# The second cross-attention's preparation done inside the self-attention before it

## The reference

```python
x = x + _L0_attn_ref(_layernorm(x), ...)            # state space
x = x + _L0_xattn_ref(_layernorm(x), ctx_768, ...)  # cross-attention, 16 heads of 64
x = x + _L0_ffn_ref(_layernorm(x), ...)             # 8 experts
x = x + _L1_attn_ref(_layernorm(x), ...)            # self-attention, 16 heads of 8, distance bias
x = x + _L1_xattn_ref(_layernorm(x), ctx_768, ...)  # second cross-attention
x = x + _L1_ffn_ref(_layernorm(x), ...)             # 8 experts
```

```python
q = layernorm(x) @ Wq; k = ctx[:, :124] @ Wk; v = ctx[:, :124] @ Wv     # 16 heads of 64
ki = ctx[:, 124:] @ Wk_ipa; vi = ctx[:, 124:] @ Wv_ipa                  # 4 "image" tokens
out = softmax(q k^T / 8) v + softmax(q ki^T / 8) vi
x = x + out @ Wo + bo
```

## Time and profile before

| | |
|---|---|
| Median of 3 runs | 705.98 us |
| Lowest, highest | 703.78, 708.40 us |
| Profiled execution | 707.48 us, of which the span from the first to the last instruction is 705.7 us |
| Mean granted TensorE clock | 0.961 of full |
| Self-attention | 302.24 us to 406.16 us of the span |
| Opening of the second cross-attention | 407.51 us to 433.72 us of the span |

### The profile page before, as it was taken

The page is one execution under the profiler, slowest core; times in us unless marked ns, Lnnn a source line. Parts: engine busy times, 40 slices in busy tenths (PEclk is TensorE's granted clock), DMA queues, the critical chain, the costliest instruction groups (busy, mean ns, idle before and its releaser), DMA issues. The chain is left out here.

```text
span 705.7 us, 13252 instructions
## 1 busy us (share of the span) xinstructions
PE 639.6 (91%) x5180; PEld 533.1 (76%) x5180; DVE 387.4 (55%) x1060; ACT 280.5 (40%) x574; POOL 195.7 (28%) x290
## 2 busy tenths in 40 slices
PE   3978997999998999978999878999999899999997
PEld 2555586888887788875666566888887688888886
DVE  3484844566657655535666353566666654444443
ACT  2585242344344233323444333445555343222321
POOL 6013610355668300020100030344366401111110
PEclk9989988999999999988999887999999999999999
DMA  7603001000000010000000020000000011111101
GB/s 191 144 1 93 9 1 46 1 2 1 2 23 24 24 45 24 1 1 1 1 2 2 1 91 2 2 1 1 3 1 1 2 46 46 46 46 45 46 1 31
DMA packets 23630, 18.50 MB, mean 26 GB/s; under 512 B 5640, under 2 KB 20368, under 8 KB 23568
## 3 DMA queue, kind: packets, MB, share of 16 engines
q1 hardware_dynamic: 23568, 17.65, 9.2%
HBM read 16.73 MB, written 0.52 MB: 24 GB/s over the span
## 5 line engine op out<-in xcount | busy, mean ns | idle before, releaser
L2519 ACT ACTIVATE sb_ca_kt<-bank 128x512 f32<-128x512 f32 x75 | 44.9, 599 | 119.1 <-PE bank L2430 118.8
L2443 PEld LDWEIGHTS bank<-sb_ff_down,sb_ca_o 128*128 128x128 f32 x768 | 88.1, 192 | 1.2
L2443 PE MATMUL bank<-sb_ff_down,sb_ca_o 128*128 128x128 f32 x768 | 88.5, 275 | 0.0
L2430 PE MATMUL bank<-sb_ff_xt_high,sb_ff_low 128*128 128x512 f32 x192 | 78.4, 408 | 5.1 <-DVE sb_ca_o L2598 2.6
L2598 DVE TENSOR_TENSOR sb_ca_o<-sb_ca_kt,bank 128x512 f32<-128x512 f32 x75 | 51.2, 686 | 55.2 <-ACT sb_ca_kt L2519 54.6
L2430 PE MATMUL bank<-sb_ff_xt_high,sb_ff_high 128*128 128x512 f32 x192 | 75.7, 394 | 0.0
L2430 PE MATMUL bank<-sb_ff_xt_low,sb_ff_high 128*128 128x512 f32 x192 | 75.4, 392 | 0.0
L1535 ACT ACTIVATE sb_shared<-bank 128x512 f32<-128x512 f32 (+1 forms) x64 | 36.0, 594 | 73.5 <-PE bank L1384 73.4
L2605 DVE SCALAR_TENSOR_TENSOR sb_x<-bank,sb_ff_cw,sb_x 128x128 f32<-128x128 f32 x128 | 35.9, 344 | 43.4 <-PE bank L2443 43.4
L1623 DVE TENSOR_REDUCE sb_ca_m<-bank 128x4 f32<-128x512 f32 (+1 forms) x64 | 40.6, 675 | 25.2 <-PE bank L1359 25.2
L1665 DVE TENSOR_TENSOR sb_ca_o<-bank,sb_ca_rinv 128x384 f32<-128x384 f32 (+1 forms) x90 | 46.2, 513 | 3.1
(11 more groups left out here) (379 smaller groups left out, 1275.2 us busy)
## 6 DMA issues: line engine op xcount, KB each, us to landing
sb_ff_w<-in_L_ffn_w_dram SPq DMA_DIRECT2D x8, 256.0 KB, 2.8
sb_ff_gate_up<-in_L_ffn_w_gate_dram SPq DMA_DIRECT2D x8, 256.0 KB, 2.7
sb_ff_gate_up<-in_L_ffn_w_up_dram SPq DMA_DIRECT2D x8, 256.0 KB, 3.0
sb_ff_down<-in_L_ffn_w_down_dram SPq DMA_DIRECT2D x8, 256.0 KB, 3.8
sb_ff_w<-in_L_ffn_w_dram SPq DMA_DIRECT2D x8, 128.0 KB, 2.8
sb_x<-in_x_dram SPq DMA_DIRECT2D x1, 512.0 KB, 4.9
sb_c_o<-in_L_xattn_w_out_dram SPq DMA_DIRECT2D x1, 512.0 KB, 7.1
sb_c_q<-in_L_xattn_Wq_dram SPq DMA_DIRECT2D x1, 512.0 KB, 4.4
```

The lines of the kernel that those rows point to most:

```text
L2430: mm = nc.tensor.matmul(ps[k % BK][:, :], wp[p][:, g, t * P:(t + 1) * P], xs[xp][:, cols], start=(q == 0), stop=(q == 2))
L2443: mm = nc.tensor.matmul(y_ps[n][:, b * D:(b + 1) * D], h[n][:, t, b * P:(b + 1) * P], down[p][:, t, :], start=(t == 0), stop=(t == FT - 1))
L2519: nc.scalar.activation(s[i % BK][:, :], gate_ps[i % BK][:, :], ACT.Silu).then_inc(act_done, 1)
```

## The change

`CrossStart` now exists for layer 1 as well and holds, beside norms, queries and keys of batches 0 and 1, the split context, the folded weights, the transposed Wv (before, in the shared probability buffer) and the values of batch 0. It is allocated ahead of the self-attention. A new class `FoldSteps` issues the work inside the self-attention: the transposes of Wv, the keys of batch 0 and the fold in its opening, all else in its last turn, through the two banks of `scores` (4 and 5). The split of the context moves to POOL's list of the self-attention, behind its last bias add. In the cross-attention the opening of layer 1 becomes that of layer 0 with image scores (in banks 6 and 7) between the scores; the transpose of the first image probabilities moves into turn 0.

```diff
+class FoldSteps:
+        uses = ["wv_t0", "wv_t1", "K00", "K01", "x", "K10", "Q00", "Q01", "K11", "Q10", "Q11", "V0", "V1", "V2", "V3"]
+    def bank(self, u):
+        return self.banks[(self.count[u] - 1) % 2]
+    def free_bank(self, pe, u):
+        if u not in ("wv_t0", "wv_t1", "x", "K10"):
+            pe.wait_ge(self.read, self.count[u] - 2)
+    def tensor_fold(self, pe, k):
+        if k:
+            pe.wait_ge(self.g_low_done, 2)
+        else:
+            pe.wait_ge(self.read, self.count["K01"])
...
+    def tensor_x(self, pe, maxima_read, count):
+        pe.wait_ge(maxima_read, count)
+        pe.wait_ge(self.xn_ready, 2)
...
+    def gpsimd_steps(self, pool):
+        nc.gpsimd.memset(s.vo[:, :, D:], 1.0).then_inc(self.ones_done, 1)
+        nc.gpsimd.tensor_copy(s.c_high[:, :, :], self.pg.ctx_t[:, 0:NB, :]).then_inc(self.c_high_done, 1)
+        pool.wait_ge(self.c_high_done, 1)
+        nc.gpsimd.tensor_tensor(s.c_low[:, :, :], self.pg.ctx_t[:, 0:NB, :], s.c_high[:, :, :], ALU.subtract).then_inc(self.c_low_done, 1)
...
@@ self_attention, tensor @@
+            steps.tensor_values_t(pe)
+            image.tensor_keys(pe)
+            for h in range(2):
+                steps.tensor_keys(pe, 0, h)
             x_transpose(0)
-            image.tensor_keys(pe)
+            steps.tensor_fold(pe, 0)
             pe.wait_ge(wt_copied, 3)
             project_q(0)
             project_k(0)
             project_v(0)
             x_transpose(1)
+            steps.tensor_fold(pe, 1)
             image.tensor_values(pe)
             project_q(1)
             project_k(1)
             project_v(1)
+            pe.wait_ge(steps.g_low_done, 4)
             scores(0, 0)
...
+            scores_t(LAST, 0)
+            steps.tensor_x(pe, s_read, NCH * NB)
+            steps.tensor_keys(pe, 1, 0)
+            values_transpose(LAST - 1)
+            steps.tensor_queries(pe, 0, 0)
+            values(LAST, 0)
+            out_transpose(LAST - 1)
+            values(LAST, 1)
+            steps.tensor_queries(pe, 0, 1)
+            scores_t(LAST, 2)
+            steps.tensor_keys(pe, 1, 1)
+            project_out(LAST - 1)
+            steps.tensor_queries(pe, 1, 0)
+            values(LAST, 2)
+            steps.tensor_queries(pe, 1, 1)
+            values(LAST, 3)
+            for q in range(2):
+                steps.tensor_values(pe, q)
+            values_transpose(LAST)
+            steps.tensor_values(pe, 2)
+            out_transpose(LAST)
+            steps.tensor_values(pe, 3)
+            project_out(LAST)
@@ self_attention, scalar, opening @@
+            steps.scalar_values_t(act)
+            for h in range(2):
+                steps.scalar_keys(act, 0, h)
             copy_xt(0)
             act.wait_ge(bias_scaled, 1)
             copy_q(0)
             image.scalar_keys(act)
+            steps.scalar_fold(act, 0)
             copy_xt(1)
+            steps.scalar_fold(act, 1)
             copy_q(1)
@@ self_attention, scalar, last turn @@
+            exp(LAST, 0)
+            exp(LAST, 1)
+            steps.scalar_x(act)
+            steps.scalar_keys(act, 1, 0)
+            copy_ot(LAST - 1)
+            steps.scalar_queries(act, 0, 0)
+            steps.scalar_queries(act, 0, 1)
+            exp(LAST, 2)
+            steps.scalar_keys(act, 1, 1)
+            exp(LAST, 3)
+            for h in range(2):
+                steps.scalar_queries(act, 1, h)
+            copy_av(LAST)
+            for q in range(2):
+                steps.scalar_values(act, q)
+            steps.scalar_values(act, 2)
+            copy_ot(LAST)
+            steps.scalar_values(act, 3)
@@ self_attention, vector @@
                 add_v(n)
                 if n == 0:
                     norm_apply(2)
+                    for k in range(2):
+                        steps.vector_fold(dve, k)
...
+                if j == LAST - 2:
+                    steps.vector_stats(dve, x_done)
+                if j == LAST - 1:
+                    steps.vector_apply(dve)
@@ cross_attention, tensor @@
             pg.wait_loads(pe, f"cross{layer}")
+            pe.wait_ge(ones_done, 3 if layer else 2)
+            scores(0, 0)
             if layer:
...
                 for n in range(2):
                     image_scores(n)
-                pe.wait_ge(img_shifted, 2)
...
@@ cross_attention, vector @@
             norm_stats(2)
             norm_aggregate(2)
+            norm_apply(2)
+            for c in range(NCH):
+                row_max(0, c)
...
+            split_max(0)
             if layer:
                 for n in range(2):
                     image_shift(n)
```

More of the change, by code:

```diff
@@ L370, in __init__ @@
         self.qt, self.kt = two("qt", [P, NT, P]), two("kt", [P, NT, P])
+        if layer:
+            self.c_high, self.c_low = (sb(f"c_{n}", [DC, NB, P], F32R) for n in ("high", "low"))
+            self.g_high, self.g_low = (sb(f"g_{n}", [DC, NH, D], F32R) for n in ("high", "low"))
+            self.vo, self.wv_t = sb("vo0", [P, NH, D + 2]), sb("wv_t", [P, NT, DC])
 class MixSteps:
@@ L1137, in cross_attention @@
         some = lambda k, n, s, dt=F32: [sb(f"{n}{p}", s, dt) for p in range(k)]
[L1138 to L1143, removed]
-        if layer:
[L1145 to L1149, removed]
+        st, mv, ve, rs = start.norm
+        xn, xt = start.xn, start.xt
+        if layer:
+            c_high, c_low, g_high, g_low = start.c_high, start.c_low, start.g_high, start.g_low
+            vo = [start.vo, sb("vo1", [P, NH, D + 2])]
+        qt, kt = [*start.qt, sb("qt2", [P, NT, P])], [*start.kt, sb("kt2", [P, NT, P])]
         m, nm, nmt = some(2, "m", [P, NH]), some(2, "nm", [P, 2, 4, NH], BF16), some(2, "nmt", [P, P], BF16)
         pt = pg.shared
-        wv_t = pt[:, 0:2, :].rearrange("p c (t d) -> p (c t) d", d=P)[:, :, 0:DC]
         rinv, o = some(2, "rinv", [P, NH]), some(2, "o", [P, NH, D])
@@ L1194, in cross_attention @@
             uses += [u for u in turn if u[1] < NB]
[L1195 removed]
+        uses = [u for u in uses if not (u[0] in "xkq" and u[1] < DONE or u[0] == "v" and (not layer or u[1] == 0))]
         count = {u: i + 1 for i, u in enumerate(uses)}
@@ L1227, in _ @@
             if layer:
[L1228 to L1233, removed]
+                nc.gpsimd.memset(vo[1][:, :, D:], 1.0).then_inc(ones_done, 1)
             rstd(2)
@@ L1460, in _ @@
                 scores_t(j, 0)
+                if layer and j == 0:
+                    image_transpose(0)
                 if ahead < NB:
@@ L1566, in _ @@
                 exp(j, 0)
+                if layer and j == 0:
+                    copy_p2(0)
                 if ahead < NB:
@@ L1686, in _ @@
                     image_shift(n)
-            for c in range(NCH):
-                row_max(0, c)
-                if c == 1:
-                    dve.wait_ge(ones_done, 4 if layer else 2)
-            split_max(0)
-            if layer:
                 for n in range(2):
@@ L1837, in self_attention @@
         image = ImageProducts(pg, ctx)
+        steps = FoldSteps(pg, start, score)
         block = ctx.enter_context(nc.Block())
```

254 lines of the change are left out of this document (140 added, 114 removed).

## The result

| | before | after |
|---|---|---|
| Median | 706.73 us (4 runs, 703.78 to 708.40) | 696.59 us (4 runs, 695.66 to 699.90) |
| Profiled execution, span | 707.48 us, 705.7 us | 699.90 us, 698.1 us |
| Mean granted clock | 0.961 | 0.967 |

The ratio is 0.988 with a 95% interval from 0.983 to 0.992: faster by over 1% as the likeliest reading, and the median lies 0.3 us from the forecast of 696.3 us. The profiled execution is the slowest of the four. Some executions of most kernels here fall into a slower state, over 1.5% above the fastest of the same kernel; ratios and medians here leave these out. That the median fell so near the forecast is in part luck: by stretch the first profiled execution is off by up to 2.7 us one way and the second, of the same code, by 1.6 us the other way.

The account below looks back on a forecast made before the run. PE's matmul time, idle time and clock were taken to bound the kernel. -19.5 + 5.7 + 4.1 = -9.7 us gave 697.8 us profiled, 696.3 us median; range with the first three rivals 691.0 to 702.0 us.

Parts of the forecast that it names:

- Part 1: Second cross-attention's opening: from 26.2 to 6.7 us, a chain through DVE as in layer 0; -19.5 us.
- Part 2: Self-attention's last turn: added PE work partly fills idle time, 11.67 to 17.4 us; +5.7 us.
- slower rival: Self-attention's last turn: clock falls early, from the wait for the first queries on; total +5.4, 711.4 us; 5%.
- Part 3: Self-attention's opening: 4.7 us of PE work added, a new 2.2 us wait at the fold's second half; +4.1 us.
- two cases: Self-attention's opening: clock falls after the new wait, +4.9 us, or stays at 2.4 GHz throughout, +1.8 us.
- my own signs of being right: Cross opening 6 to 8 us; last turn 16 to 19, clock 1.00; first scores 2 to 5 later, wait about 2.
- Part 4: Turns and queues: POOL's split in turn 4, SP queue and first cross turn cost 0 us.
- my rival with the clock up: Clock holds in the self-attention's opening (+1.8) and the first cross turn saves 1: -13.0, 693.0 us; 19%.
- port rival: Turn 4: POOL's split holds DVE's cast of the maxima, bias add 1.9 us late; +1.2, total -8.5, 697.5 us; 7%.

Follow-up runs that it names:

- the two undone halves: Changed kernel with fold, first keys and values back in the cross-attention's opening (703.01 us), or instead norms, queries and second keys back there (697.90 us).
- best: Changed kernel with second fold in banks 2 and 3, both cross-opening waits cut, POOL's context split in the self-attention's opening; 691.10 us, ratio 0.972 to 0.983.
- norm_late: Changed kernel with only the norm of batch 2 put behind the second row maximum in the cross-attention's opening; 699.06 us, one run.
- nowait: Changed kernel with only the scores of batch 1 freed from waiting for the image shifts in the cross-attention's opening; 695.10 us, one run.
- dve_order: Changed kernel with batch 2's norm behind the second row maximum and batch 1's scores not waiting for the image shifts; 690.58 us, one run.
- again: Changed kernel measured once more with no edit; 692.08 us, ratio to the kernel before 0.982 (0.977 to 0.986).
- banks: Changed kernel with the second half of the fold in banks 2 and 3, so it waits for no subtraction; 688.24 us, ratio 0.971 to 0.982.
- banks_split: Changed kernel with second fold in banks 2 and 3 and POOL's context split in the self-attention's opening; 691.56 us, ratio 0.973 to 0.984.
- fill: Changed kernel with seven unread matmuls on PE ahead of the second half of the fold; 693.01 us, ratio 0.977 to 0.987.
- wait_doubled: Changed kernel with two memsets on DVE ahead of its subtractions, lengthening PE's wait by 1.9 us; 699.52 us, ratio 0.989 to 0.997.

## Why the prediction was right, and where it was not

- **Part 1, the cross-attention's opening: -19.5 forecast, -20.1 measured.** Right in size and in mechanism; DVE's chain sets its length, as in layer 0. That the norms and the fold both have to leave it for this to hold is shown by the two undone halves.
- **Part 2, the last turn: +5.7 forecast, +5.0 measured.** The clock was 1.00 in every execution with the change, so the slower rival has nothing for it. The wait for the first queries was 0.18 us, not 0.4, and of the 1.0 us of chain at the end little was left, since the last values lie in it: PE was busy for 16.16 of the 16.68 us.
- **Part 3, the self-attention's opening: +4.1 forecast, +6.8 in the first execution, +2.5 in the second.** The term was mis-sized, and it was the mean of two cases (+4.9 and +1.8), so that no single execution could show it. The wait at the second half of the fold came as worked out (1.87 us against 2.2, released by DVE's subtraction). But with the clock down I had put 3 us on what runs behind it, 4.9 in all; measured are 27.25 - 22.99 = 4.3 us, since the image values alone grew from 2.00 to 3.67 us and the slow stretch reached from the wait past the first scores, 10.2 us. And with the clock up I had +1.8, where 2.5 us were measured. To the first scores, the mark of the forecast, it is +6.5 (20.70 us for 14.19) and +2.1 (16.27 us); the rest lies behind that mark, where I had put nothing. So of my own signs of being right one failed in the first execution: first scores 2 to 5 us later. I had given the falling clock three times the chance of the holding one; in six profiled executions it fell twice, which is too few to put a better chance on it.
- **Part 4, turns and queues: 0 forecast; +0.3 us in the self-attention's turns, -0.5 in the first cross turn (9.86 us before, 9.39 after, by the same marks).** In the second execution the turns took 72.66 us for 71.80 before, 0.9 more: the slow stretch that began 2.3 us before the opening's end reached far into the first turn, where the first 16 us ran at 0.75 and not 0.79. Part of what the opening saves is handed back there.
- **The sum.** First execution: -20.1 + 5.0 + 6.8 + 0.3 - 0.5 = -8.5 us, for -9.7 forecast; my rival with the clock up, forecast at -13.0, is the second execution with -12.1. The median fell between them and on the forecast, which is luck as far as it goes below 1 us; the repeated measurement of the same kernel gave 692.08, nearer the rival's 693.0, and both lie in the range.
- **The port rival** was right in mechanism and wrong in victim and price. The views of turn 4 in the first execution:

```profile
379.07 1.03 POOL L1869 CAST sb_ca_c_high<-sb_ctx_t 96x1024 fp32r<-96x1024 f32 x1
380.07 0.20 DVE L2266 CAST sb_sa_nm<-sb_sa_m 128x64 bf16<-128x64 f32 x1
380.19 2.35 POOL L1871 TENSOR_TENSOR sb_ca_c_low<-sb_ctx_t,sb_ca_c_high 96x1024 fp32r<-96x1024 f32 x1
380.30 2.32 DVE L2268 TENSOR_TENSOR sb_sa_nm<-sb_sa_m,sb_sa_nm 128x64 bf16<-128x64 f32 x1
382.54 0.68 DVE L2272 TENSOR_TENSOR sb_sa_pre<-bank,sb_shared 128x512 f32<-128x512 f32 x1
```

  The cast of the maxima was not held (0.20 us). The subtraction behind it was, for 2.32 us, until POOL's own was done. In best, where the split lies elsewhere, the eight instructions of that line take 225 ns in the mean; in after 487 ns, which is one of eight held for 2.1 us. It cost the turns 0.3 us (72.10 for 71.79), not the 1.2 us that I had worked out. The bias add behind it started 2.24 us after it, for 1.09 us in best, so it came 1.15 us late and not 1.9, and by difference PE's cover took 0.85 of these and not 0.7. That the cast was free says little, as POOL's own cast ended 0.03 us after it began. The Trainium skill, SBUF — State Buffer, "Who interferes with whom", has the case: a DVE instruction with two inputs in SBUF contends with a GpSimd instruction that reads SBUF. This row agrees; my estimate looked at the page's other case, casts.

## What to carry to other kernels

Work that stands in a chain at the start of a stage can be cheap in the tail of the stage before it, where another chain leaves PE idle: here the values cost nothing there. Give a moved step its own buffer or bank, or the reuse of a bank becomes a wait at the new place, and price that wait with the clock up and with the clock down, since the same code did both here. Compare stretches that begin at the same instruction before believing a median, and check the stretch behind a saving: here a wait cut from a short opening came back, with interest, in the next turn.

## What was not expected of the hardware

- The same opening with the same 1.87 us wait at the same place kept the 2.4 GHz clock past the wait in four executions and lost it in two; the difference is 4.3 us in the opening, of which 0.6 us went back in the turns behind it.
- Code that no edit touched took 296.5 to 308.0 us ahead of the self-attention, at granted clocks of 0.98 and 0.94.
- Shortening the idle time of the cross-attention's opening by 0.6 to 1.5 us went with a longer stretch at 1.2 GHz: 10.2 us in three kernels (norm_late, nowait, dve_order) and 13.6 in best, where after, again, banks, banks_split, fill and wait_doubled all have 6.8 us. The cross-attention's opening and first turn of best and dve_order are the same code, so the code alone does not set the length.
- One DVE subtraction of 128 x 64 elements, 0.23 us otherwise, stood for 2.32 us beside a POOL subtraction of 2.35 us. DVE's two row maxima (378.75 to 380.04 us, read from PSUM) took 1.29 us beside POOL's cast, as they do without it in best.
